# Spreading B for VectorE's states by one bf16 pass over three parts of the fp32 row, in a Mamba and mixture-of-experts layer on one core

## The reference, cut to what matters

```python
# x: 8 sequences x 512 tokens x 256 channels; d_inner 512, d_state 16
h = silu(causal_conv4(layernorm(...) @ in_proj_w.T))          # 512 channels
proj = h @ x_proj_w.T
dt_in, B, C = proj[..., :1], proj[..., 1:17], proj[..., 17:33]
dt = softplus(dt_in @ dt_proj_w.T + dt_proj_b)
# for each token t, channel d and state n
state[d, n] = exp(-exp(A_log[d, n]) * dt[t, d]) * state[d, n] + B[t, n] * h[t, d]
y[t, d]     = sum_n state[d, n] * C[t, n] + D[d] * h[t, d]
out = silu(y) @ out_proj_w.T + shortcut
# then x + layernorm(out), and a top-1 mixture of 8 experts with one shared expert
```

## Time and profile before

| | |
|---|---|
| median of 3 runs | 1578.79 us (1577.54 to 1582.05) |
| the profiled execution, its own time | 1582.94 us |
| its span, first to last instruction | 1581.0 us |
| PE busy | 1205.1 us (76%) |
| DVE busy | 1040.5 us (66%) |
| POOL busy | 1026.3 us (65%) |
| ACT busy | 800.2 us (51%) |
| TensorE's mean granted clock | 0.900 of 2.4 GHz |
| GpSimd's weighing of states (L483), first to last start | 110.1 to 1064.2 us of the span |

### The profile page before, as it was taken

The page is one execution under the profiler, slowest core; times in us unless marked ns, Lnnn a source line. Parts: engine busy times, 40 slices in busy tenths (PEclk is TensorE's granted clock), DMA queues, the critical chain, the costliest instruction groups (busy, mean ns, idle before and its releaser), DMA issues. The chain is left out here.

```text
span 1581.0 us, 15574 instructions
## 1 busy us (share of the span) xinstructions
PE 1205.1 (76%) x4766; PEld 530.7 (34%) x4767; DVE 1040.5 (66%) x1049; ACT 800.2 (51%) x1376; POOL 1026.3 (65%) x477
## 2 busy tenths in 40 slices
PE   2456587796886876986886886764999989999950
PEld 1121121331331322321322331323555556666630
DVE  2149899899899889899899899791311112323237
ACT  2445656776776865865866866444111111111127
POOL 0049999999999999999999999980361000000025
PEclk9889799999999989889989887876999999999985
DMA  2160130240140140122122122012952021111135
GB/s 56 55 249 1 55 134 0 69 159 2 69 150 10 56 148 27 56 97 76 46 88 82 38 95 83 1 54 93 374 188 68 2 76 40 46 40 46 40 102 180
DMA packets 77953, 128.46 MB, mean 81 GB/s; under 512 B 7616, under 2 KB 56384, under 8 KB 73792
## 3 DMA queue, kind: packets, MB, share of 16 engines
q1 hardware_dynamic: 67120, 108.93, 20.5%
q10 hardware_dynamic: 7696, 10.36, 1.9%
q0 software_dynamic: 3072, 8.39, 1.7%
HBM read 95.94 MB, written 31.72 MB: 81 GB/s over the span
## 5 line engine op out<-in xcount | busy, mean ns | idle before, releaser
L483 POOL TENSOR_TENSOR state<-state,cbc 128x1024 f32<-128x1024 f32 x256 | 611.8, 2410 | 14.4 <-DVE state L956 14.3
L956 DVE TENSOR_TENSOR_SCAN state<-psX,bx 128x1024 f32<-128x1024 f32 x256 | 577.8, 2278 | 57.8 <-ACT psX L694 32.3
L694 ACT ACTIVATE psX<-dt,aneg 128x511 f32<-128x511 f32 x512 | 330.8, 679 | 222.2 <-DVE state L956 220.7
L1233 PE MATMUL psY<-state,ident 64*64 64x512 f32 x2048 | 294.0, 667 | 47.9 <-POOL state L483 47.9
L472 POOL TENSOR_TENSOR bx<-xh,bbc 128x1024 f32<-128x1024 f32 x128 | 309.2, 2416 | 29.7 <-DVE state L956 29.7
L550 POOL DMA_INDIRECT fy<-slot_out,slot x32 | 33.0, 1031 | 341.7 <-DMA slot_out<-yo 332.3
L1225 PE MATMUL bank<-prow,ident 128*128 128x512 f32 x256 | 161.0, 714 | 114.5 <-DVE bx L944 114.4
L944 DVE TENSOR_TENSOR bx<-xh,bank 128x1024 f32<-128x1024 f32 x128 | 153.0, 1195 | 0.0
L1233 PEld LDWEIGHTS psY<-state,ident 64*64 64x64 f32 x2048 | 65.3, 142 | 240.3 <-issue 127.7
L1065 DVE TENSOR_TENSOR actN<-sg,psX 128x512 f32<-128x512 f32 x39 | 26.8, 688 | 142.1 <-ACT sg L791 142.1
L1225 PEld LDWEIGHTS bank<-prow,ident 128*128 128x128 f32 x256 | 46.4, 216 | 203.8 <-DVE bx L944 159.6
(11 more groups left out here) (145 smaller groups left out, 1578.8 us busy)
## 6 DMA issues: line engine op xcount, KB each, us to landing
cbc<-bc_rows SPq DMA_DIRECT2D x32, 1024.0 KB, 4.9
bbc<-bc_rows SPq DMA_DIRECT2D x16, 1024.0 KB, 6.0
slot_in<-ao SPq DMA_DIRECT2D x1, 4992.0 KB, 26.8
xsl<-slot_in SPq DMA_DIRECT2D x39, 128.0 KB, 2.2
slot_out<-yo ACTq DMA_DIRECT2D x39, 128.0 KB, 2.4
xin<-in_x SPq DMA_DIRECT2D x8, 512.0 KB, 4.2
xr<-in_x SPq DMA_DIRECT2D x8, 512.0 KB, 6.0
x_rows<-ao SPq DMA_DIRECT2D x8, 512.0 KB, 2.9
```

Of the source, the lines that this page charges most:

```text
L483: nc.gpsimd.tensor_tensor(w[:], w[:], cbc[:, n].unsqueeze(1).broadcast_to([P, CH, L]), ALU.mult).then_inc(weighted, 1)
L694: e = nc.scalar.activation(decay[q % RD][:, c, 1:L], dt[par][:, h * CH + c, 1:L], ACT.Exp, scale=aneg[:, h * CH + c, n:n + 1])
L956: nc.vector.tensor_tensor_scan(st[q % RS][:].rearrange("p c t -> p (c t)"), decay[q % RD].rearrange("p c t -> p (c t)"), bx[q % RB][:].rea ...
L1233: done = nc.tensor.matmul(psY[o * HP:(o + 1) * HP, r], weights(half, c), src[half, c], start=first, stop=last_)
```

## The change

A new bf16 tensor `pick_row` (128 x 16) has a one on partitions n, 64 + n and 96 + n of column n. It is made of the identity by two additions at the start on VectorE, with a semaphore between them, ahead of dD and `setup`.

Each front has a new step `split` on VectorE at q = 15, behind scan(15) and ahead of scan(16). It waits for `prow_kept`. Its first instruction subtracts from partitions 64 to 127 of `prow` their own upper 16 bits, read as bf16 with a stride of two, so there the row's first rest remains. After a semaphore the second does the same on partitions 96 to 127, where the second rest remains. The upper halves of the three copies (the row, its first rest, its second rest) add up to the fp32 row.

The spread is a matmul of `pick_row`'s column with the upper halves of all of `prow`, both bf16, in one pass. Its first in each iteration waits for `parts_ready`, which split's second instruction signals, in place of `prow_kept`. SyncE's store still waits for `prow_kept`; it reads partitions 0 to 31, which split doesn't touch.

```diff
--- before.py
+++ after.py
@@ -101,6 +101,7 @@
         hT = lt[:, C // 2:C]
         dD = sb("dD", [P, C, HP], where=A)
         minus = sb("minus", [P, P], where=A)
+        pick_row = sb("pick_row", [P, N], BF16, where=A)
         yv = sb("yv", [P, C, L], where=A)
         xin = sb("xin", [P, J, DIM], where=A)
         xr = sb("xr", [P, J, DIM], where=A)
@@ -189,6 +190,7 @@
         consts = sem("consts_loaded")
         slots_zeroed = sem("slots_zeroed")
         ident_made = sem("ident_made")
+        pick_made = sem("pick_made")
         setup = sem("setup")
         aexp = sem("aexp")
         zeroed = sem("zeroed")
@@ -221,6 +223,8 @@
         dtin_ready = sem("dtin_ready")
         proj_ready = sem("proj_ready")
         prow_kept = sem("prow_kept")
+        rest_ready = sem("rest_ready")
+        parts_ready = sem("parts_ready")
         z_done = sem("z_done")
         u_ready = sem("u_ready")
         lt_ready = sem("lt_ready")
@@ -294,6 +298,9 @@
         xst_v = xs_d.rearrange("(t p) c -> t p c", p=P)
         yt_v = y_d.rearrange("(t p) c -> t p c", p=P)
         outp_v = out.rearrange("b (q h p) c -> (b q) p h c", p=P, h=2)
+
+        def upper_half(rows):
+            return rows.bitcast(BF16).rearrange("p (t two) -> p two t", two=2)[:, 1]
 
         def pick(v, i):
             return v[bass.ds(i, 1)].rearrange("a p c -> p (a c)") if len(v.shape) == 3 else \
@@ -855,6 +862,9 @@
                 nc.vector.tensor_copy(w_bc[:, :, g, :], xp[:, :, 1:1 + G3])
             dve.wait_ge(ident_made, 2)
             nc.vector.tensor_scalar(minus[:], ident[:], -1.0, None, ALU.mult)
+            nc.vector.tensor_tensor(pick_row[:], ident[:, 0:N], ident[:, HP:HP + N], ALU.add).then_inc(pick_made, 1)
+            dve.wait_ge(pick_made, 1)
+            nc.vector.tensor_tensor(pick_row[:], pick_row[:], ident[:, HP + 2 * N:HP + 3 * N], ALU.add).then_inc(pick_made, 1)
             for r in range(2):
                 half = slice(r * HP, (r + 1) * HP)
                 nc.vector.tensor_tensor(dD[half], ident[half, half].unsqueeze(1).broadcast_to([HP, C, HP]),
@@ -893,6 +903,13 @@
                     if not (isinstance(f, int) and f < 2):
                         dve.wait_ge(mv_ready[0], f - 1)
                     stats(0, cl, f, xin, mv0[par], mv0_ready)
+
+            def split(f, par):
+                dve.wait_ge(prow_kept, f + 1)
+                first, second = prow[par][HP:P], prow[par][HP + 2 * N:P]
+                nc.vector.tensor_tensor(first, first, upper_half(first), ALU.subtract).then_inc(rest_ready, 1)
+                dve.wait_ge(rest_ready, f + 1)
+                nc.vector.tensor_tensor(second, second, upper_half(second), ALU.subtract).then_inc(parts_ready, 1)
 
             def front(f, par, q):
                 if q in (3, 5, 7, 9):
@@ -907,6 +924,8 @@
                             last.then_inc(conv_done, 1)
                         else:
                             cf.link(f, last)
+                if q == 15:
+                    split(f, par)
                 if q in (23, 24):
 
 
@@ -1219,10 +1238,12 @@
             def spread_b(i, par, q):
                 n = q % N
                 if q == 1:
-                    pe.wait_ge(prow_kept, i + 1)
+                    pe.wait_ge(parts_ready, i + 1)
+                    if isinstance(i, int) and i == 0:
+                        pe.wait_ge(pick_made, 2)
                 if not (isinstance(i, int) and i == 0 and q == 1):
                     pe.wait_ge(dve_bx, i * DQ + q // 2)
-                nc.tensor.matmul(psB[:], ident[:, n:n + 1].broadcast_to([P, P]), prow[par][:],
+                nc.tensor.matmul(psB[:], pick_row[:, n:n + 1].broadcast_to([P, P]), upper_half(prow[par][:]),
                                  start=True, stop=True).then_inc(b_bcast, 1)
 
             def tiles(src, weights, first, last_):
```

## The result

The changed kernel takes 1598.61 us (median of 4, 1596.45 to 1601.14), the kernel before 1579.01 beside it: ratio 1.0125, 95% interval 1.0102 to 1.0148. It is slower by 19.6 us; 1595.4 was forecast. Two repetitions on other occasions gave 1.0145 (1.0125 to 1.0166) and 1.0137 (1.0120 to 1.0154).

What follows compares the result with a forecast made beforehand. GpSimd was taken as the bound, VectorE setting the pace for a few steps after q = 15. Iterations 1 to 6 (12.7), iteration 0 (3.3) and start (0.6) sum to 16.6 us: 1595.4 from 1578.79, range 1582 to 1606.

Steps and rivals of the forecast that it cites:

- The spread at 0: TensorE's spread: one bf16 pass for the fp32 pair frees 0 to 161 us of TensorE, worth 0 in run time.
- The start at 0.6: Ahead of setup: two small additions and a semaphore wait cost 0.6 us, bounds 0.3 and 1.0.
- The first subtraction goes at 403.8 ... and pushes weigh(15)'s end: Iteration 2, after weigh(14): VectorE's first subtraction is let in, moving weigh(15)'s end from 406.1 to 406.6.
- the other one, at +0.4 an iteration: At q = 15: both subtractions run only once GpSimd has run out of work, resuming at 407.5, +0.4 us each iteration.
- the forecast form: At q = 15: first subtraction enters after weigh(14), 1 to 3 us; second waits for weigh(15), about 2.7 us.
- TensorE's second projection isn't late: Iteration 2, second L1195: starts about 1.5 us after the first L925, ends 416.3, before VectorE comes at 416.7.
- that mechanism among the rivals, with 6%: Output projections: more TensorE idle time brings 1.2 GHz, projections take 7.4 us, +4.8 in six iterations, 1624; chance 0.06.
- my formula: Iterations 1 to 6: delay is inject(20)'s start minus L925's, both before the change, plus 3.85 us; sum 12.7.
- Iteration 0 at 3.3: Iteration 0, without L925 or idle time to use up: inject(20) starts 3.3 us later; bounds 0 and 3.3.
- The lock: VectorE instructions with two SBUF inputs wait for GpSimd's running one and delay its next, 0.5 us at 512 columns.
- No lock: Rival at the split: subtractions don't wait for GpSimd, nothing is late, 0 to +3 us, 1576 to 1582; chance 0.10.
- Faster: Rival: without GpSimd blocking, TensorE's relief brings projections forward, at most -1.9 us in six iterations, 1567; chance 0.04.

Runs made afterwards that it cites:

- the spread alone: The changed kernel without the split, spreading only the upper half of B's row in one bf16 pass, against the kernel before: 0.9990, -1.3 us.
- split alone: The changed kernel with both subtractions but the old fp32 two-pass spread, against the kernel before: 1.0138, +20.7 us.
- the two runs with a busier TensorE: The changed kernel with the old fp32 spread (1.0138), and with each bf16 spread issued three times (1.0155), each against the kernel before.
- the run with PSUM inputs: The changed kernel with both subtractions' first operand read from PSUM instead of prow (output wrong), against the kernel before: 0.9964.
- the spread three times over: The changed kernel with each bf16 spread issued three times into the same bank, against the kernel before: 1.0155, median 1608.0 us.

## Why the prediction was right, and where its steps weren't

The sign, the place and the mechanism were right: two-SBUF-input subtractions that wait for GpSimd hold up scan(16), and GpSimd then stands idle for it. The size was 16.6 us forecast and 19.6 measured, and that it came so near is in part luck: two steps failed upwards, and two stretches that the sum had at nothing gave 3.6 us back. In the trace, the start of GpSimd's weigh(15) and weigh(19) in each iteration, after against before, gives the terms one by one. For iteration 2: from 403.79 to 419.73 before, 15.94 us; from 410.13 to 428.84 after, 18.71; hence 2.8.

| term | forecast | in the trace |
|---|---|---|
| start, up to the first weigh | +0.6 | -0.4 |
| iteration 0 | +3.3 | +3.8, and 1.1 ahead of weigh(15) |
| iterations 1 to 6 | 2.1, 1.8, 2.2, 1.7, 1.8, 3.1: 12.7 | 4.4, 2.8, 3.2, 1.9, 2.0, 3.3: 17.5 |
| elsewhere | 0 | -2.5 (iteration 0, later), -1.1 (between 3 and 4) |
| sum, at the last weigh | 16.6 | 18.4 |

- *The spread at 0*: right. L963 idle 0.0, and the spread alone at 0.9990. By busy time TensorE got back 102 of the 161 us of the passes, nearer to two thirds of them than to three quarters.
- *The start at 0.6*: not to be seen; the first weigh starts 0.4 us earlier than before.
- *"The first subtraction goes at 403.8 ... and pushes weigh(15)'s end"*: this step failed. In iterations 1 and 2 it was passed over at the end of weigh(14). In 0 and 3 to 6 weigh(15) was already running when prow came, by 0.1 to 0.5 us. In all seven GpSimd ran dry first, so L490 wasn't made longer (2414 ns on average against 2410) and the second subtraction took 0.69 us in place of my 2.7. I had prow ready 0.5 us ahead of weigh(14)'s end, as before; why it came later than that in five of the seven iterations isn't shown. The case stood in the text as the other one, at +0.4 an iteration, and that is what came: resumption at 413.8 where 407.5 plus the 6.35 us by which iteration 2 was late at weigh(15) gives 413.85. Split at q = 28 shows the forecast form, 2.73 and 2.80 us, and so do three iterations of split alone at q = 15.
- *"TensorE's second projection isn't late"*: this failed too, and it is the larger part of what is missing. It took 5.5, 5.0 and 4.6 us in iterations 1 to 3 of this trace, and 4.1 to 5.5 in all six of the second trace of the change. Part of it ran at 1.2 GHz, in a stretch that follows on the 3.54 us in which TensorE now waits for VectorE between the two projections. I had that mechanism among the rivals, with 6%, at both projections and at full length; it came at one, in part. Iteration 1 is the clearest: 4.4 where my formula and 0.4 give 2.5, and where the two runs with a busier TensorE lost 2.3 and 2.2. By their traces the slow projections of iterations 1 to 3 cost 2.1, 0.8 and 0.8 us, 3.7 in all; no comparison of medians shows it. The wait between the projections doesn't do it by itself, since the clock held in those two runs after 2.92 and 3.15 us of it in iteration 2; what else it takes is not shown.
- *Iteration 0 at 3.3*: 3.8. The 1.1 us ahead of its weigh(15) are in the trace of the spread alone as well, so they aren't split's. Afterwards 2.5 us came back, because L916 (here L935) was let in after 1.34 us, where it had waited 8.25 before. I had put that into the lower bound.
- *The lock*: right in kind. *No lock*: refuted by the subtractions of 2.5 to 4.6 us beside GpSimd, against 0.69 us with a PSUM input. *Faster*: refuted for this change. That its mechanism, projections that come earlier once the spread is cheap, is what made the run with PSUM inputs 5.5 us faster than before is not shown.

The two profiled executions differ by 13.5 us in span (1581.0 and 1594.5) and 18.4 at the last weigh. That of before took 1582.94 us, above all the timed runs of its kernel, that of after 1596.45, the lowest of its four, and the 4.9 us between lie behind the Mamba part, spread over the expert stages; their cause is open.

What stays open is what decides whether GpSimd or VectorE goes next when both are ready. Over all traces, instructions of VectorE with two SBUF inputs that came 0.1 to 2.9 us before the end of the running GpSimd instruction were passed over, and others that came 0.1 to 2.3 us before it were let in. What GpSimd did next, a product or a weighing, doesn't tell them apart either.

## What to carry to other kernels

Before moving work to VectorE beside a busy GpSimd, count its SBUF inputs: with one of them in PSUM the subtractions cost nothing here, even with a copy more (1.0004), with both in SBUF 20 us. The price of such an instruction isn't its duration but the scan queued behind it, up to the time at which GpSimd runs out of work, so it belongs where GpSimd's next instructions don't hang on what VectorE does next (q = 28: +7 in place of +20). And a pass that nobody waits for (idle time 0.0 ahead of its reader) is worth little however much it shrinks: 100 us of TensorE's busy time gave 1.3, by the interval 3 at most.

## What the runs showed of the hardware that I had not expected

- A VectorE instruction with two SBUF inputs that waits for GpSimd may be passed over several times: 7.1 to 7.9 us in the split at q = 16, with two or three whole GpSimd instructions between. "SBUF — State Buffer" of the Trainium skill (section "Who interferes with whom") has the second blocked until the first is finished; these runs agree that it is blocked, and don't agree that one instruction is all that it waits for.
- A bf16 pass whose moving operand is read with a stride of two runs at about the price of one without it: where the clock held, the passes of the spread three times over follow each other in 0.22 to 0.24 us (the Trainium skill, "TensorE: Matmul & The Clock Gate", section "Back-to-back issue gap", gives 216 ns for an isolated pass of 512 columns; no run here has a bf16 pass without the stride to set beside it). As a row of the profile such a pass takes 385 to 400 ns.
- A subtraction of 32 partitions takes as long as one of 64: 0.69 us both.
